# Delta rule stage: queries and keys projected once, the four-tap convolution done on ScalarE and VectorE

## The reference, cut to what matters

```python
def _causal_dw_conv_silu(x, w):                       # w: (channels, 4)
    C = x.shape[-1]
    y = jax.lax.conv_general_dilated(jnp.swapaxes(x, 1, 2), w[:, None, :], window_strides=(1,),
                                     padding=[(KS - 1, 0)], feature_group_count=C)
    return jax.nn.silu(jnp.swapaxes(y, 1, 2))
...
q = _causal_dw_conv_silu(x @ Wq, conv_q).reshape(bsz, seq_len, H, KD)     # H = 8, KD = 128
k = _causal_dw_conv_silu(x @ Wk, conv_k).reshape(bsz, seq_len, H, KD)
v = _causal_dw_conv_silu(x @ Wv, conv_v).reshape(bsz, seq_len, H, VD)     # VD = 32
q = _l2norm(q); k = _l2norm(k)
# then, token by token: state = a (state - b (state k) k^T) + b v k^T, out = state q
```

## Time and profile before

| | |
|---|---|
| runs of the kernel before | 4292.37 us median of 3 (4273.81 to 4297.87) |
| the profiled execution | 4287.15 us, span 4285.4 us |
| mean granted TensorE clock | 0.859 |
| busy over the span | PE 3686.3 us (86%), PEld 2276.7 (53%), DVE 2300.0 (54%), ACT 1558.3 (36%), POOL 761.2 (18%) |
| L2129, the taps | x1024 records, busy 545.8 us |

### The profile page before, as it was taken

One profiled execution on the slowest core, in us unless ns is written; L12 is line 12 of the kernel. 1 busy time (PEld: TensorE's weight loads), 2 busy tenths in 40 slices (PEclk: granted clock), 3 DMA queues, 4 the chain that ended last, 5 costly groups with the idle time before them and its releaser, 6 DMA issues. The chain is left out here.

```text
span 4285.4 us, 124546 instructions
## 1 busy us (share of the span) xinstructions
PE 3686.3 (86%) x55640; PEld 2276.7 (53%) x55640; DVE 2300.0 (54%) x5899; ACT 1558.3 (36%) x2877; POOL 761.2 (18%) x724
## 2 busy tenths in 40 slices
PE   3877776689898888998876987999999999999986
PEld 2336664235554455554554433666666666666672
DVE  3757775267667666676672112444444444444445
ACT  2653333363344443444210433333333333333323
POOL 1212221011112111122110001222222222222210
PEclk9886667798888888988655998999999999999967
DMA  2000000221111111110000000000000000000000
GB/s 83 0 0 1 1 1 1 75 62 37 41 33 41 44 33 39 39 42 27 3 3 17 0 21 40 2 3 2 2 2 2 2 2 3 2 2 2 2 3 22
DMA packets 37030, 79.22 MB, mean 18 GB/s; under 512 B 7568, under 2 KB 11025, under 8 KB 35345
## 3 DMA queue, kind: packets, MB, share of 16 engines
q1 hardware_dynamic: 36496, 71.25, 5.1%
HBM read 66.91 MB, written 4.33 MB: 17 GB/s over the span
## 5 line engine op out<-in xcount | busy, mean ns | idle before, releaser
L2129 PE MATMUL ps<-d_hp,d_w_qk 128*128 128x512 f32 x1024 | 545.8, 629 | 2.7 <-DVE d_hp L2386 2.7
L1388 PE MATMUL ps<-g_hs,g_fc 128*128 128x512 f32 x448 | 289.8, 733 | 82.0 <-ACT g_hidden L1510 75.9
L1510 ACT ACTIVATE g_hidden<-ps 128x512 f32<-128x512 f32 x224 | 133.1, 594 | 377.5 <-PE ps L1388 377.5
L2207 POOL TENSOR_TENSOR d_sq<-d_QK 128x512 f32<-128x512 f32 x128 | 133.0, 1039 | 759.5 <-ACT d_QK L2249 754.1
L1402 PE MATMUL ps<-g_hidden,g_proj 128*128 128x512 f32 x448 | 263.6, 685 | 0.0
L1279 PEld LDWEIGHTS ps<-g_Q,g_K 32*32 32x32 f32 x12288 | 193.9, 113 | 130.1 <-issue 46.6
L1279 PE MATMUL ps<-g_Q,g_K 32*32 32x32 f32 (+1 forms) x12288 | 224.9, 218 | 28.1 <-DVE g_H L1548 12.0
L1229 POOL TENSOR_TENSOR g_tmp<-g_rs 128x512 f32<-128x512 f32 x16 | 26.7, 1667 | 1029.9 <-ACT g_rs L1468 1029.9
L2227 ACT ACTIVATE d_F<-ps 128x128 f32<-128x128 f32 x256 | 70.8, 276 | 381.0 <-PE ps L2043 379.9
L2129 PEld LDWEIGHTS ps<-d_hp,d_w_qk 128*128 128x128 f32 x1024 | 162.5, 190 | 81.9 <-issue 63.4
L1388 PEld LDWEIGHTS ps<-g_hs,g_fc 128*128 128x128 f32 x448 | 82.4, 217 | 191.5 <-ACT g_hidden L1510 144.6
(11 more groups left out here) (473 smaller groups left out, 8009.2 us busy)
## 6 DMA issues: line engine op xcount, KB each, us to landing
g_hs<-gate_rows SPq DMA_DIRECT2D x56, 256.0 KB, 3.5
g_fc<-in_c_fc_dram SPq DMA_DIRECT2D x56, 256.0 KB, 3.9
g_proj<-in_c_proj_dram SPq DMA_DIRECT2D x56, 256.0 KB, 2.8
d_QK<-in_conv_qk_dram SPq DMA_DIRECT2D x2, 2048.0 KB, 6.8
X<-in_x_dram SPq DMA_DIRECT2D x1, 2048.0 KB, 11.0
w_c_fc<-in_c_fc_dram SPq DMA_DIRECT2D x1, 2048.0 KB, 7.8
w_c_proj<-in_c_proj_dram SPq DMA_DIRECT2D x1, 2048.0 KB, 12.2
ex_root<-gate_rows SPq DMA_DIRECT2D x1, 2048.0 KB, 15.0
```

Source lines behind the costliest of these rows:

```text
L1388: e.matmul(P[2], fc[:, n % 2, ts(f, C)], hs[:, n % 2], start=True, stop=True).then_inc(pe.steps, pe.did(now(f"u{i}")))
L1510: e.activation(r[:, slot], P[2], ACT.Relu).then_inc(act.steps, act.did(now(f"r{i}")))
L2129: ins = e.matmul(b, w_qk[:, j, c, ts(H, C)], hp_of(u)[:, j:j + T], start=(j == 0), stop=(j == TAPS - 1))
L2207: e.tensor_tensor(squares(x), qk, qk, ALU.mult).then_inc(pool.steps, pool.did(f"{tag}sq{x}"))
```

## The change

The weights scaled by taps, their two blocks, and the load of the plain weights inside `delta_start` go. `Wqk3` and the taps as a per-partition table `conv_qk3` are loaded with the group "delta". A run becomes one matmul of the plain weights against the unshifted input; ScalarE copies the bank to a new tile `convolved` times the last tap (conv piece j = 0), and VectorE adds the three other taps, one scalar_tensor_tensor each, from the same bank shifted by 1, 2 and 3 columns (j = 1, 2, 3), each waiting for the one before. Silu then reads `convolved` instead of PSUM.

```diff
-        w_qk = k.sb("d_w_qk", [C, TAPS, 2, 8 * C], stack=s)
+        convolved = k.sb("d_conv", [C, 2, T], stack=s)
...
-                e.dma_start(w_plain, k.dram["Wqk3"]).then_inc(dma.steps, dma.did("plain"))
-                e.wait_ge(dma.steps, dma.at("plain"))
...
-        for n in range(2):
-            pe, act, dve, pool, dma = k.stage(f"delta_taps{n}")
-                    e.dma_start(taps, src.to_broadcast([C, TAPS, 8 * C])).then_inc(dma.steps, dma.did("taps"))
-                    for j in range(TAPS):
-                        e.tensor_tensor(w_qk[:, j, n], w_plain[:, n], taps[:, j], ALU.mult).then_inc(dve.steps, dve.did())
...
                 for x in range(32):
                     turn = NI * (x // 8) - 50 + x % 8
-                    put(u, turn, "taps", x, place={8: 0, 0: 0, 1: 1}.get(turn % NI, 2))
+                    if x % 8 == 0:
+                        put(u, turn - 1, "taps", x)
+                    elif x % 8 == 4:
+                        put(u, turn, "taps", x)
+                for x in range(8):
+                    for j in range(TAPS):
+                        put(u, NI * (x // 2) - (50, 45)[x % 2] + (0, 0, 1, (3, 2)[x % 2])[j], "conv", TAPS * x + j, place=(1 if j == 0 else 2))
...
-                            ins = e.matmul(b, w_qk[:, j, c, ts(H, C)], hp_of(u)[:, j:j + T], start=(j == 0), stop=(j == TAPS - 1))
+                            if u or run > 1:
+                                e.wait_ge(dve.steps, dve.at(f"{tag}conv{TAPS * run - 5}" if run > 1 else f"u{u - 1}conv{27 + 4 * c}"))
+                            e.matmul(b, k.w["Wqk3"][:, c, ts(H, C)], hp_of(u)[:, 3:3 + T], start=True, stop=True).then_inc(pe.steps, pe.did(f"{tag}run{run}"))
...
+                        elif what == "conv" and x % TAPS == 0:
+                            e.wait_ge(pe.steps, pe.at(f"{tag}run{run}"))
+                            e.activation(convolved[:, c], tap_bank(run), ACT.Copy, scale=k.w["conv_qk3"][:, c, 4 * g + run // 2, 3:4]).then_inc(act.steps, act.did(f"{tag}conv{x}"))
...
-                            e.activation(QK[:, x % 2, 4 * (u % 3) + x // 2], tap_bank(x), ACT.Silu).then_inc(act.steps, act.did(f"{tag}run{x}"))
+                            e.wait_ge(dve.steps, dve.at(f"{tag}conv{TAPS * x + 3}"))
+                            e.activation(QK[:, x % 2, 4 * (u % 3) + x // 2], convolved[:, x % 2], ACT.Silu).then_inc(act.steps, act.did(f"{tag}run{x}"))
...
+                        elif what == "conv" and x % TAPS:
+                            if late == 1:
+                                e.wait_ge(act.steps, act.at(f"{tag}conv{TAPS * run}"))
+                            else:
+                                e.wait_ge(dve.steps, dve.at(f"{tag}conv{x - 1}"))
+                            cv = convolved[:, run % 2, late:]
+                            e.scalar_tensor_tensor(cv, tap_bank(run)[:, 0:T - late], k.w["conv_qk3"][:, run % 2, 4 * g + run // 2, 3 - late:4 - late], cv,
+                                                   ALU.mult, ALU.add).then_inc(dve.steps, dve.did(f"{tag}conv{x}"))
```

More of the change, by code:

```diff
@@ L123 @@
     "gla": ["W_in2", "b_in2", "W_qka", "b_qka", "W_v2", "b_v2", "W_y2", "b_y2", "W_out2", "b_out2", "h0", "gla_mask"],
-    "delta": ["Wv3", "Wg3", "Wab3", "Wo3", "A_log", "dt_bias", "conv_v", "o_norm_w", "joins", "eye32", "upto3", "ones3", "picks"],
+    "delta": ["conv_qk3", "Wqk3", "Wv3", "Wg3", "Wab3", "Wo3", "A_log", "dt_bias", "conv_v", "o_norm_w", "joins", "eye32", "upto3", "ones3", "picks"],
     "mix": ["W_r3", "W_k3", "W_v3", "mu"],
@@ L1873, in delta_rule @@
         pe, act, dve, pool, dma = k.stage("delta_start")
-        w_plain = QK[:].rearrange("p c h t -> p (c h t)")[:, 20 * T:].rearrange("p (c f) -> p c f", c=2)
         with nc.Block() as block:
-            @block.sync
-            def _(e):
-                e.dma_start(w_plain, k.dram["Wqk3"]).then_inc(dma.steps, dma.did("plain"))
-                e.wait_ge(dma.steps, dma.at("plain"))
             @block.scalar
@@ L1892, in delta_rule @@
         k.end()
-        taps = QK[:].rearrange("p c h t -> p (c h t)")[:, 0:TAPS * 8 * C].rearrange("p (j f) -> p j f", j=TAPS)
-        for n in range(2):
-            pe, act, dve, pool, dma = k.stage(f"delta_taps{n}")
[L1896 to L1899, removed]
-                    e.dma_start(taps, src.to_broadcast([C, TAPS, 8 * C])).then_inc(dma.steps, dma.did("taps"))
-                @block.vector
-                def _(e):
-                    e.wait_ge(dma.steps, dma.at("taps"))
-                    for j in range(TAPS):
-                        e.tensor_tensor(w_qk[:, j, n], w_plain[:, n], taps[:, j], ALU.mult).then_inc(dve.steps, dve.did())
-            k.end()
         f2 = lambda ap: ap.rearrange("p h t -> p (h t)")
@@ L2126, in prepare @@
                                 e.wait_ge(dve.steps, dve.at(f"u{u - g}nh"))
-                            if j == 0 and (u or run > 1):
-                                e.wait_ge(act.steps, act.at(f"{tag}run{run - 2}" if run > 1 else f"u{u - 1}run{run + 6}"))
-                            ins = e.matmul(b, w_qk[:, j, c, ts(H, C)], hp_of(u)[:, j:j + T], start=(j == 0), stop=(j == TAPS - 1))
-                            if j == TAPS - 1:
-                                ins.then_inc(pe.steps, pe.did(f"{tag}run{run}"))
+                            if u or run > 1:
+                                e.wait_ge(dve.steps, dve.at(f"{tag}conv{TAPS * run - 5}" if run > 1 else f"u{u - 1}conv{27 + 4 * c}"))
+                            e.matmul(b, k.w["Wqk3"][:, c, ts(H, C)], hp_of(u)[:, 3:3 + T], start=True, stop=True).then_inc(pe.steps, pe.did(f"{tag}run{run}"))
                         elif what == "squares":
@@ L2246, in prepare @@
                                          ACT.Silu).then_inc(act.steps, act.did(f"{tag}values{x}"))
+                        elif what == "conv" and x % TAPS == 0:
+                            run = x // TAPS
+                            e.wait_ge(pe.steps, pe.at(f"{tag}run{run}"))
+                            c = run % 2
+                            if u or run > 1:
+                                e.wait_ge(act.steps, act.at(f"{tag}run{run - 2}" if run > 1 else f"u{u - 1}run{6 + c}"))
+                            e.activation(convolved[:, c], tap_bank(run), ACT.Copy, scale=k.w["conv_qk3"][:, c, 4 * g + run // 2, 3:4]).then_inc(act.steps, act.did(f"{tag}conv{x}"))
                         elif what == "taps_done":
-                            e.wait_ge(pe.steps, pe.at(f"{tag}run{x}"))
-                            e.activation(QK[:, x % 2, 4 * (u % 3) + x // 2], tap_bank(x), ACT.Silu).then_inc(act.steps, act.did(f"{tag}run{x}"))
+                            e.wait_ge(dve.steps, dve.at(f"{tag}conv{TAPS * x + 3}"))
+                            e.activation(QK[:, x % 2, 4 * (u % 3) + x // 2], convolved[:, x % 2], ACT.Silu).then_inc(act.steps, act.did(f"{tag}run{x}"))
                         elif what == "gate" and x == 0:
@@ L2386, in prepare @@
                             e.tensor_scalar(hp_of(u)[:, 3:], tmp[:, 0, :], k.mod[:, 3, CA, b:b + 1], k.mod[:, 3, SA, b:b + 1], ALU.mult, ALU.add).then_inc(dve.steps, dve.did(tag + "nh"))
+                        elif what == "conv" and x % TAPS:
+                            run, late = x // TAPS, x % TAPS
+                            if late == 1:
[5 more added lines that the diff above has]
+                                                   ALU.mult, ALU.add).then_inc(dve.steps, dve.did(f"{tag}conv{x}"))
                         elif what == "scale":
@@ L2706, in layouts @@
     o["Wqk3"] = c(np.stack([i["L3_attn_Wq"], i["L3_attn_Wk"]], 1))
-    o["conv_qk"] = c(np.stack([i["L3_attn_conv_q"].T, i["L3_attn_conv_k"].T], 0))
+    o["conv_qk3"] = c(np.stack([i[f"L3_attn_conv_{n}"].reshape(8, C, 4).transpose(1, 0, 2) for n in "qk"], 1))
     o["Wv3"] = c(i["L3_attn_Wv"])
```

## The result

The changed kernel takes 4367.34 us (median of 4 runs, 4358.04 to 4375.26) where the kernel before takes 4295.12 on the same chip: ratio 1.0171, interval [1.0123, 1.0219]. It is slower by 1.7%, some 73 us; 4255 had been forecast, with a range to 4345. The profiled execution has a span of 4364.4 us and a mean granted clock of 0.779, against 0.859.

A forecast was written before the change was run, and what follows sets the result against it. TensorE (PE), busy 98 of 100 us in the delta stage's loop, was taken as the bound. 4287 - 25.5 (staging) - 160 (matmuls removed) + 157 (lower clock) - 3 (double counting) gave 4255 us, range 4140 to 4345.

The forecast's parts named there:

- Ahead of the loop: Before the delta stage's first matmul: two blocks of weight staging go, gain 25.5 us, between 22 and 28.
- The work that leaves PE and the gaps it leaves: In the loop: 5.16 us of matmuls go per chunk, idle PE grows 2.4; gain 160 us at full clock.
- The steps: VectorE steps at turn ends: 1.2 us a chunk on PE's path from W's wait; the even run's cost nothing.
- rival 3: In the loop: new steps cost more than their place, VectorE as bound; up to +190 us, a part 4313; chance 0.1.
- The clock: In each chunk, 1.2 GHz from turns 0 to 2 through the even run's matmul: 2.7 us a chunk, 157 us.
- rival 2: Low clock lasts through turns 8 and 0: 4.4 us a chunk; 4319 (one in four), 4383 (one in two); chance 0.18.
- The sample at the loop's end: Kernel before, from 4060 us, where the loop runs without taps: clock 0.71, L2074 3.4 us instead of 1.7.
- The sum: Whole program: 4287 - 25.5 - 160 + 157 = 4258.5, less 3 for a clock drop counted twice; forecast 4255.

The follow-up runs named there:

- with filler: The changed kernel plus three matmuls a chunk of 512 columns on constant operands, at the ends of turns 0, 1 and 7: 4179 us, ratio 0.9727.

## Why the prediction was wrong

**Ahead of the loop: right.** 25.5 us were forecast; the kernel with four matmuls and no steps gives 29 (20 to 38), and in the trace of the changed kernel the first L2012 group starts 26.9 us earlier.

**The work that leaves PE and the gaps it leaves: right in kind.** The waits for X (1.29), ze (0.46) and W (0.92) stand where the prediction put them, with about its sizes (1.4, 0.46, 1.2). PE's idle time was forecast to grow by 2.4 us a chunk, and it grew by 2.4, from 23.99 - 23.61 = 0.38 to 25.95 - 23.18 = 2.77. The forecast of 160 us at full clock can't be tested alone, since no kernel here with one matmul a run has the full clock without filler; with filler, whose own cost is included, the loop gives 2.7% less the staging's 0.7%, 88 us.

**The steps: about right.** 1.2 us a chunk was the forecast for those on the path; 1.8% over 64 chunks is 1.2 us, 1.4% is 0.9. The wait for W, which the forecast had as 1.2, is 38.4 us over some 50 chunks, 0.8 a chunk; where the rest of the steps' cost lies wasn't found. The even run's steps were held to cost nothing, and rival 3's sign was PE waiting for steps in turns 4 to 7. In the whole trace PE waited for a step once, 1.4 us; weight loads of L2020 did so 44 times, 19.9 us in all, while PE was busy. What the even run's steps cost wasn't measured apart; moving the odd run's earlier gave back half.

**The clock: the step that failed, by its length.** The prediction let 1.2 GHz begin in turns 0 to 2 and end with the even run's matmul, 2.7 us a chunk, 157 us. It does end there. But it begins in turn 8, so that the state product (+1.6 us), L2012 (+1.0) and the odd run's matmul (+0.4) are paid too. The squares were also priced too low within the forecast's own stretch: half of them, two records, cost 2 x 0.43 = 0.86 at the low level and not 0.4, and the chunk shows +0.85. With +0.93 for L2020 and +0.95 for the even run's matmul these are 5.7 us, by the same groups in the chunk with filler. (The 5.9 us between the two chunks are these, about 1 us in the small groups and 1.8 of waits, less 2.9 for three fillers.)

On average it is less than in this chunk. PE's busy time should have fallen by the 5.16 us of the twelve records that left; it fell by 23.61 - 23.18 = 0.43. So the clock cost about 4.7 us a chunk, an estimate from the busy times of the traces, where 2.7 had been forecast. Over 58 chunks the 2.0 us between them are 116 us. That is nearly the whole miss of 112: from the first L2012 group to the last the loop takes 1601.4 us where it took 1491.8, +110, and the forecast's terms for it were -160 + 157 - 3 = -6.

This is rival 2's mechanism and place, and its sign, L2074 (now L2058) at 3.4 us a group, came. It had been given 0.18, with 4319 for one chunk in four and 4383 for one in two. That the measured 4367 lies near the second is in part luck: 31 of 38 state products are at the low level, and not half of them, and a chunk then pays less than rival 2's 4.4 us, since "finish" stays at the high level (1.08 and 1.06 us for L2076 and L2080 in the chunk shown).

Its weight was too small because of a sentence about place: that the odd run's matmul "stands just there, and is dense". It stands behind "finish", and a stretch that had become sparse is ahead of it, in turns 6 to 8, from which tap matmuls had gone as well: the earlier trace rows show four records right ahead of L2092. I had looked at one sparse stretch of the chunk and there were two. With the odd run's matmul inside that stretch, in turn 7, 34 of 41 state products are at the high level or near it, where it was 7 of 38. The sample at the loop's end pointed there: L2074 was already at the low level.

**The sum.** The forecast gain at full clock and the forecast cost of the clock were of the same size, 160 and 157 us, so an error in either could turn the sign. The difference of two such terms has the spread of both, and the range's upper end should have been taken from rival 2's second price, 4383.

The rule of the Trainium skill that the prediction weighed ("TensorE: Matmul & The Clock Gate", section "Why this matters for your kernels"), that the clock holds as long as there are no idle gaps of some microseconds, would have kept 2.4 GHz here. The longest wait in the chunk shown is 1.3 us, the longest between 2700 and 4000 us is 1.5, and the clock there is 0.75; the measurement decides, as the sample had.

## What to carry to other kernels

Before dense matmuls are taken off a TensorE that is the bound, look at how the kernel's own sparse stretches are clocked; such a matmul costs its own time, and may keep up the clock of its neighbours. If the clock falls, a busy share near 90% hides it, since the same work is busy for longer: compare the duration of one unchanged group at both levels. Then try the place before the amount, since one matmul moved by a turn gave 2.2% here, and a matmul that serves nothing, put into a gap, is a fair experiment and can be a fair kernel.

## What the runs showed of the hardware that was not expected

Busy time alone doesn't hold the clock: PE at 92% (1195.28 of 1300 us, one matmul and no steps) had 0.76, and at 91% (1188.70 of 1300, two fillers and moved runs) 0.95. What differs is which matmuls fill the time and where. And a VectorE step with both tensors in SBUF took 737 ns where GpSimd was idle and 1320 on average, up to 1760, where it overlapped an instruction of GpSimd; with one operand in PSUM it took 733 and 744.
